# A 16-head linear attention and three further layers on one core: the first segment's way to the first products rearranged

## The reference, cut to what matters

```
qkv  = silu(x_normed @ w_qkv.T)          # 16 heads of 128, q, k, v
per block:  o = (q * q_decay) @ state + (q @ k.T * decay) @ v
            state = decay * state + (k * k_decay).T @ v
out  = rmsnorm(o);  gate = sigmoid(x_normed @ w_gate.T);  (gate * out) @ w_out.T
```

## Time and profile before

| | us |
|---|---|
| median of 3 runs | 1204.62 |
| the runs | 1197.87 to 1205.65 |
| span of the profiled execution | 1198.6 |

### The profile page before, as it was taken

One profiled execution on the slowest core, in us unless ns is written; L12 is line 12 of the kernel. 1 busy time (PEld: TensorE's weight loads), 2 busy tenths in 40 slices (PEclk: granted clock), 3 DMA queues, 4 the chain that ended last, 5 costly groups with the idle time before them and its releaser, 6 DMA issues. The chain is left out here.

```text
span 1198.6 us, 19843 instructions
## 1 busy us (share of the span) xinstructions
PE 1134.0 (95%) x7044; PEld 993.3 (83%) x7044; DVE 756.3 (63%) x1600; ACT 513.5 (43%) x969; POOL 240.8 (20%) x274
## 2 busy tenths in 40 slices
PE   5999999999999999999999996889999779989997
PEld 4988988988989889889898995667776668878897
DVE  4765665666656647657567578754445975786656
ACT  5576344344443443444434555422222356554322
POOL 1012010110100101101001002033332742322211
PEclk9999999999999999999999997899999958999999
DMA  4001001000001001001000003733333324000001
GB/s 149 10 1 36 10 1 36 9 0 35 9 0 40 4 0 44 0 0 44 0 0 1 1 2 120 228 93 106 106 106 91 95 82 146 1 1 1 19 18 36
DMA packets 29212, 50.33 MB, mean 42 GB/s; under 512 B 5122, under 2 KB 19426, under 8 KB 27874
## 3 DMA queue, kind: packets, MB, share of 16 engines
q1 hardware_dynamic: 24978, 38.68, 9.8%
q0 software_dynamic: 3840, 10.49, 3.3%
q10 hardware_dynamic: 336, 0.39, 0.1%
HBM read 36.70 MB, written 10.49 MB: 39 GB/s over the span
## 5 line engine op out<-in xcount | busy, mean ns | idle before, releaser
L635 POOL TENSOR_TENSOR linear_out_row<-linear_out_row,lin_sq 128x512 f32<-128x512 f32 x64 | 91.3, 1426 | 598.7 <-ACT lin_sq L536 595.7
L42 PE MATMUL lin_bank<-keep_xT_hi,lin_w_hi 128*128 128x512 f32 x384 | 155.4, 405 | 2.6 <-DVE keep_xT_lo L244 2.6
L591 DVE TENSOR_TENSOR lin_st<-lin_bank,lin_mask 128x512 f32<-128x512 f32 x64 | 44.3, 692 | 174.9 <-PE lin_bank L446 174.9
L43 PE MATMUL lin_bank<-keep_xT_lo,lin_w_hi 128*128 128x512 f32 x384 | 152.6, 397 | 0.0
L44 PE MATMUL lin_bank<-keep_xT_hi,lin_w_lo 128*128 128x512 f32 x384 | 152.5, 397 | 0.0
L532 ACT ACTIVATE lin_o<-lin_bank 128x512 f32<-128x512 f32 x64 | 38.3, 598 | 189.9 <-PE lin_bank L477 189.9
L473 PE MATMUL lin_bank<-lin_st,lin_v 128*128 128x128 f32 x512 | 94.0, 275 | 0.0
L42 PEld LDWEIGHTS lin_bank<-keep_xT_hi,lin_w_hi 128*128 128x128 f32 x384 | 72.9, 190 | 17.9 <-issue 3.0
L44 PEld LDWEIGHTS lin_bank<-keep_xT_hi,lin_w_lo 128*128 128x128 f32 x384 | 72.5, 189 | 17.8
L477 PE MATMUL lin_bank<-lin_qd,lin_state 128*128 128x128 f32 x448 | 87.2, 276 | 0.0
L43 PEld LDWEIGHTS lin_bank<-keep_xT_lo,lin_w_hi 128*128 128x128 f32 x384 | 72.8, 189 | 14.8
(11 more groups left out here) (395 smaller groups left out, 2775.9 us busy)
## 6 DMA issues: line engine op xcount, KB each, us to landing
lin_raw<-in_wp SPq DMA_DIRECT2D x8, 1024.0 KB, 4.8
sorted_y<-shared_loaded SPq DMA_DIRECT2D x48, 128.0 KB, 2.1
experts_up_expert_up<-in_wgu SPq DMA_DIRECT2D x16, 352.0 KB, 7.2
keep_x<-in_x SPq DMA_DIRECT2D x4, 512.0 KB, 7.3
lin_raw_out<-in_wop SPq DMA_DIRECT2D x8, 256.0 KB, 2.6
tokens_x<-linear_out_row SPq DMA_DIRECT2D x4, 512.0 KB, 10.6
linear_out_row<-in_ffn_up SPq DMA_DIRECT2D x2, 1024.0 KB, 5.9
tail_q<-tail_qT SPq DMA_DIRECT2D x28, 64.0 KB, 2.0
```

The costliest lines, as they stand in the source:

```text
L42: nc.tensor.matmul(out, lh, rh, start=first, stop=False, skip_group_check=skip)
L43: nc.tensor.matmul(out, lh, rl, start=False, stop=False, skip_group_check=skip)
L591: dve.tensor_tensor(C4(st[:, a, :]), C4(bank[2 + a][:]), mask[:, a:a + 1, :].broadcast_to([P, TPS, P]), ALU.mult).then_inc(st_sb, 1)
L635: pool.tensor_tensor(part, part, sq[:, a, :], ALU.add).then_inc(squares_sb, 1)
```

## The change

- The four tiles of segment 0 are issued as four transfers with a semaphore each, ahead of everything; the slopes are issued by ScalarE instead of SyncE. `raw` arrives in two transfers by column halves (0 to 511: q0, k0, q1, k1; 512 to 1023: g, v), both ahead of the norm weights and segment 1.
- `dve_first` takes each tile's statistics as it arrives, and normalizes tiles 2 and 3; `act_first` normalizes tiles 0 and 1. `pe_turn_first` waits for VectorE's tiles before the block that needs them.
- Both splits of the weights go by column halves, in every pass. In the first, half 0 is split before `act_high` and `dve_low`, half 1 after.
- `project_first` writes q0 of segment 0 in another order, each product waiting for its own parts: high by high for both feature halves, low weights by high, high by low. `pe_pass` waits for the second half of the weights only before v.
- The slopes' negation (L148) moves behind the second half of the weights on VectorE.
- TensorE first makes `WARM` = 12 products of the identity with itself into bank 7, which g1's first product overwrites: six whole, six in two halves of 64 output partitions each.

The diff, without the parts that only pass names on:

```diff
 RMS_EPS, LN_EPS = 1e-6, 1e-5
 PAIRS = NH // 2
 DMA = 16
+WARM = 12
 def three_passes(nc, out, lhs, rhs, first=True, last=True, skip=False):
...
     def dve_start(self, dve):
         dve.wait_ge(self.numbered, 4)
         dve.tensor_scalar(self.ages[:], self.ages[:], 0.0, None, ALU.max).then_inc(self.ready, 1)
+    def dve_slopes(self, dve):
         dve.wait_ge(self.slopes_in, DMA)
         dve.tensor_scalar(self.neg[:], self.slopes[:], -1.0, None, ALU.mult).then_inc(self.ready, 1)
...
                         z.then_inc(self.z_y_ready, 1)
                 chain.wait()
+    def dve_first(self, dve, chain, arrived):
+        at = slice(TPS, 2 * TPS)
+        for j in range(TPS):
+            dve.wait_ge(arrived[j], DMA)
+            chain.step(dve.bn_stats(self.stats[:, TPS + j, :], self.keep.x[:, j, :]))
+        chain.wait()
+        for j in range(TPS):
+            chain.step(dve.bn_aggr(self.mean_var[:, TPS + j, :], self.stats[:, TPS + j, :]))
+        chain.wait()
+        dve.tensor_scalar(self.spread[:, at], self.mean_var[:, at, 1], LN_EPS, None, ALU.add).then_inc(self.spread_ready, 1)
+        dve.wait_ge(self.root_ready, 1)
+        chain.link(dve.reciprocal(self.scale[:, at], self.root[:, at]))
+        dve.scalar_tensor_tensor(self.shift[:, at], self.mean_var[:, at, 0], -1.0, self.scale[:, at], ALU.mult, ALU.mult).then_inc(self.affine_ready, 1)
+        for j in range(TPS // 2, TPS):
+            last = dve.tensor_scalar(self.z_x(0)[:, j, :], self.keep.x[:, j, :], self.mean_var[:, TPS + j, 0:1], self.scale[:, TPS + j:TPS + j + 1],
+                                     ALU.subtract, ALU.mult)
+        last.then_inc(self.z_x_dve, 1)
+    def act_first(self, act):
+        act.wait_ge(self.affine_ready, 1)
+        for j in range(TPS // 2):
+            last = act.activation(self.z_x(0)[:, j, :], self.keep.x[:, j, :], ACT.Identity,
+                                  scale=self.scale[:, TPS + j:TPS + j + 1], bias=self.shift[:, TPS + j:TPS + j + 1])
+        last.then_inc(self.z_x_ready, 1)
+    def pe_turn_first(self, pe):
+        pe.wait_ge(self.z_x_ready, 1)
+        for k in range(KT):
+            for j in range(TPS):
+                if k == 0 and j == TPS // 2:
+                    pe.wait_ge(self.z_x_dve, 1)
+                last = pe.transpose(self.banks[k][:, j * P:(j + 1) * P], self.z_x(0)[:, j, k * P:(k + 1) * P], self.keep.ident[:])
+            last.then_inc(self.turned, 1)
     def dve_low(self, dve, g):
         for k in range(KT):
             dve.wait_ge(self.high, KT * g + k + 1)
...
                                         (keep.xT_hi[:, f, toks], keep.xT_lo[:, f, toks]), f == 0, f == KT - 1)
                 return last
-            pe.wait_ge(w_hi_done, 2 * hp + 2)
-            pe.wait_ge(w_lo_done, 2 * hp + 2)
+            def project_first():
+                cols, toks = slice(0, P), slice(0, SEG)
+                pe.wait_ge(w_hi_done, 1)
+                for f in range(KT):
+                    pe.wait_ge(norms.high, f + 1)
+                    nc.tensor.matmul(bank[0][:], w_hi[:, f, cols], keep.xT_hi[:, f, toks], start=f == 0, stop=False)
+                pe.wait_ge(w_lo_done, 1)
+                for f in range(KT):
+                    nc.tensor.matmul(bank[0][:], w_lo[:, f, cols], keep.xT_hi[:, f, toks], start=False, stop=False)
+                for f in range(KT):
+                    pe.wait_ge(norms.low, f + 1)
+                    last = nc.tensor.matmul(bank[0][:], w_hi[:, f, cols], keep.xT_lo[:, f, toks], start=False, stop=f == KT - 1)
+                return last
+            if not first:
+                pe.wait_ge(w_hi_done, 2 * hp + 2)
+                pe.wait_ge(w_lo_done, 2 * hp + 2)
             for seg in range(SEGS):
                 t = 4 * hp + seg
                 start = first and seg == 0
-                if first:
+                if first and seg:
                     pe.wait_ge(norms.low, KT * (seg + 1))
                 if not start:
                     pe.wait_ge(o_sb, 2 * t - 1)
-                project("q", 0, bank[0], seg).then_inc(q_mm, 1)
+                (project_first() if start else project("q", 0, bank[0], seg)).then_inc(q_mm, 1)
                 if not start:
                     pe.wait_ge(o_sb, 2 * t)
                 project("k", 0, bank[1], seg).then_inc(k_mm, 1)
...
                 if not start:
                     pe.wait_ge(st_sb, 2 * t)
                 project("k", 1, bank[3], seg).then_inc(k_mm, 1)
+                if start:
+                    pe.wait_ge(w_hi_done, 2)
+                    pe.wait_ge(w_lo_done, 2)
                 for b in range(2):
                     if not (first and seg <= 1):
                         pe.wait_ge(acc_sb, 2 * t - 3 + b)
...
                                         (g_hi[:, a, :], g_lo[:, a, :]), a == 0, a == 1)
                 last.then_inc(w_mm, 1)
+        HALVES = (slice(0, 512), slice(512, 1024))
         def act_split(act, hp):
             act.wait_ge(raw_in, DMA * (hp + 1))
-            for f in range(KT):
-                act.activation(w_hi[:, f, :], raw[:, f, :], ACT.Copy).then_inc(w_hi_done, 1)
+            for half in HALVES:
+                act.activation(w_hi[:, :, half], raw[:, :, half], ACT.Copy).then_inc(w_hi_done, 1)
+        def act_split_first(act, n):
+            act.wait_ge(raw_in if n else raw_half, DMA)
+            act.activation(w_hi[:, :, HALVES[n]], raw[:, :, HALVES[n]], ACT.Copy).then_inc(w_hi_done, 1)
         def act_pass(act, hp, first, last):
             for seg in range(SEGS):
...
                 chain.link(dve.tensor_copy(g_hi[:, a, :], g[:, a, :]))
                 dve.tensor_tensor(g_lo[:, a, :], g[:, a, :], g_hi[:, a, :].bitcast(F32), ALU.subtract).then_inc(g_sb, 1)
+        def dve_split_half(dve, hp, n):
+            dve.wait_ge(w_hi_done, 2 * hp + 1 + n)
+            half = HALVES[n]
+            dve.tensor_tensor(w_lo[:, :, half], raw[:, :, half], w_hi[:, :, half].bitcast(F32), ALU.subtract).then_inc(w_lo_done, 1)
         def dve_split(dve, hp):
-            for f in range(KT):
-                dve.wait_ge(w_hi_done, 2 * hp + 1 + f)
-                dve.tensor_tensor(w_lo[:, f, :], raw[:, f, :], w_hi[:, f, :].bitcast(F32), ALU.subtract).then_inc(w_lo_done, 1)
+            for n in range(2):
+                dve_split_half(dve, hp, n)
         def accumulate(dve, t, seg):
...
         with nc.Block() as block:
             @block.sync
             def _(sp):
-                decays.load(sp, slope)
                 tiles = x.rearrange("b (t p) f -> p (b t) f", p=P)
-                for g in range(SEGS):
+                for j in range(TPS):
+                    sp.dma_start(keep.x[:, j, :], tiles[:, j, :]).then_inc(x_first[j], DMA)
+                sp.dma_start(raw[:, :, HALVES[0]], w_pairs[0][:, :, HALVES[0]]).then_inc(raw_half, DMA)
+                sp.dma_start(raw[:, :, HALVES[1]], w_pairs[0][:, :, HALVES[1]]).then_inc(raw_in, DMA)
+                sp.dma_start(norm_in[:], norm_w).then_inc(norm_sem, DMA)
+                for g in range(1, SEGS):
                     at = slice(g * TPS, (g + 1) * TPS)
                     sp.dma_start(keep.x[:, at, :], tiles[:, at, :]).then_inc(x_in[g], DMA)
-                    if g == 0:
-                        sp.dma_start(raw[:], w_pairs[0]).then_inc(raw_in, DMA)
-                        sp.dma_start(norm_in[:], norm_w).then_inc(norm_sem, DMA)
                 sp.dma_start(raw_out[:], wout_pairs[0]).then_inc(raw_out_in, DMA)
                 with sp.Fori(0, PAIRS - 1) as hp:
                     sp.wait_ge(w_lo_done, 2 * hp + 2)
...
                 chain = Chain(dve, own)
                 norms_chain = Chain(dve, norms_own)
                 decays.dve_start(dve)
-                dve_norms(dve, norms_chain, 1)
-                dve_split(dve, 0)
+                norms.dve_first(dve, norms_chain, x_first)
+                dve_split_half(dve, 0, 0)
                 norms.dve_low(dve, 0)
+                dve_split_half(dve, 0, 1)
+                decays.dve_slopes(dve)
                 dve_norms(dve, norms_chain, 2)
                 dve.memset(output.ones[:], 1.0).then_inc(output.ones_ready, 1)
                 chain.link(dve.memset(keep.acc[:], 0.0))
...
             @block.scalar
             def _(act):
+                decays.load(act, slope)
                 norms.act_root(act, 1)
-                norms.act_apply(act, 1)
-                act_split(act, 0)
+                norms.act_first(act)
+                act_split_first(act, 0)
                 norms.act_high(act, 0)
+                act_split_first(act, 1)
                 norms.act_root(act, 2, split=False)
                 norms.act_apply(act, 2)
                 decays.act_start(act)
...
             @block.tensor
             def _(pe):
                 pe.wait_ge(decays.numbered, 5)
-                norms.pe_turn(pe, 0)
+                for n in range(WARM):
+                    if n < WARM // 2:
```

(5 more changed lines are left out.)

6 lines of the change are left out of this document (4 added, 2 removed).

## The result

| | before | changed |
|---|---|---|
| median, 20 runs each | 1200.49 us | 1196.76 us |
| the runs | 1197.11 to 1205.65 | 1192.91 to 1198.71 |
| span of the profiled execution | 1198.6 us | 1191.6 us |

The ratio of the changed kernel to the one before is 0.9963, with a 95% interval from 0.9953 to 0.9972: 4.4 us gained, between 3.4 and 5.6 (the two medians in the table are 3.7 apart). The forecast was 5.0. The median of the first three runs of before, 1204.62, lay 4 us above that of twenty.

The account below looks back on a forecast made before the run. TensorE, busy 95% of 1198.6 us, was taken as the bound, leaving only its start to shorten: 5.2 us arriving less 0.2 lost gives 5.0, hence 1199.6 against the 1204.62 median, taken as 1199; range 1192 to 1204.5.

Parts of the forecast that it names:

- S: Start of the kernel, moment the first segment's four statistics end: claimed 5.0 us instead of 6.6, 1.6 us gained.
- Rival A: Start: ScalarE's, little comes through; fourth tile takes 3.9 us or overwritten products end at 9.8; some 2.9 us left, 1202; chance 0.20.
- Normalization, weights, transposed parts: Start: shared normalization saves 1.0 us more before transposes; half the weights ahead of first products; seventh product about 11.2, not 17.34.
- V: Start of the products of `lin_v` and `lin_kd` (L457 before): claimed 25.85 us instead of 31.04.
- What is late next: ScalarE's fixed order behind segment 1's statistics: 2 us become a wait for ScalarE, 5.2 us arrive.
- Rival B: Start: all of TensorE's gain arrives, 7.3 us, giving 1197; needs ScalarE's exponentials or table loads out of the way; chance 0.08.
- The overwritten products: TensorE's idle start: twelve products end between 7.3 and 9.8 us; loss taken as 0.2, between nothing and 2.5.
- the 0.5 worked out: TensorE's start: if the clock rises only at 16.2 us, 4.7 us are gained instead of 5.2.
- The clock: TensorE's start: up at the seventh product gives 5.2 us; if transposes don't count and the warm-up is lost, 4.7.
- The sum's own size, 5.0: Whole kernel: 5.2 us arriving from the start less 0.2 for the overwritten products; forecast case's chance 0.50.
- Rival C: Later stages: slower, as the clock falls to 1.2 GHz in more stretches; ten such microseconds eat the gain, twenty give 1209; chance 0.15.
- Rival D: Start: the change doesn't do what it says, clock low until 25.7 us, time as before, 1204.6; chance 0.07.

Follow-up runs that it names:

- same half twice: Changed kernel with the twelve half-width overwritten products all on output partitions 0 to 63 instead of alternating halves; products of `lin_v` and `lin_kd` start at 26.60 us.
- slopes on SyncE: Changed kernel with x's first segment and the first weights in one transfer each, slopes issued first by SyncE; products of `lin_v` and `lin_kd` start at 27.30 us.
- x one, weights one: Changed kernel with x's first segment in one transfer and the first weights in one transfer; products of `lin_v` and `lin_kd` start at 30.63 us.

## Why the prediction was right, point by point

*The time.* The gain came as forecast, 4.4 us where 3.5 to 6 was said. The time of 1199 was built on a median of three runs that lay 4 us high; the measured 1196.76 is below the 1198 to 1201 that went with the forecast, and inside the wide range of 1192 to 1204.5.

*S.* Predicted 5.0, measured 5.25. The fourth tile landed 2.6 us after its issue (2.4 assumed). The price nearly stood; its reasons didn't. I counted the slopes' move as 0.46 us of SyncE and the tiles as one statistic instead of four. The runs show that each was measured wrongly by itself: the tiles with the slopes on SyncE bring 0.5 us of S (6.51 to 6.02), the slopes' move another 0.8, and the slopes' move without the tiles loses 3.2. That the sum of two wrong reasons came near is luck. Rival A had this danger as competition with the weights; in the runs it went with the slopes.

*Normalization, weights, transposed parts.* Predicted and measured: transposes 7.5 and 7.71, high weights 7.4 and 7.55, second low part 10.9 and 11.04, seventh product 11.2 and 11.44. VectorE's two tiles took 0.73 us, inside ScalarE's 1.09. One thing went unpriced: the first half of the weights landed 4.7 us after its issue, at 7.4, 0.2 before ScalarE took it up at 7.55. In the run with the same half twice it was 0.56 us too late, and V with it.

*What is late next.* Segment 1's statistics at 12.15 and 12.17, `lin_q` at 21.13 and 21.17, the transposes of `lin_k` at 22.3 and 22.31, V at 25.85 and 25.87, all in the row of ScalarE's fixed order. The run with the exponentials early showed that this order, and no other thing, keeps 1.8 us back. Rival B needed exactly this and is excluded for the change as it is.

*The overwritten products.* They ended at 7.78, transposes were ready at about the same time, and nothing was lost: 0 of the 0.2 assumed and the 2.5 feared, because the halves overlap. What they bring is up to 0.56 us (0.18 of it scatter in S), against the 0.5 worked out, and that agreement is luck. The 0.5 stood for a clock that rises at 16.2 and makes TensorE itself late; without the products it rose before 12.5, and the loss came by the transposes and ScalarE's chain. The sum was off as well: transposes of `lin_k` ready at 23.4 and the 2.66 us from there to the products of `lin_v` and `lin_kd` give 26.1, a loss of 0.2 and not 0.5.

*The clock.* Here a step was missing. I weighed the clock only as up or down at the seventh product, and took the order by parts as worth nothing beyond its place. In the run with the old order a wait of 2.61 us there is followed by a low clock from 12.2 to 15.6. The rule that transposes do not count (the Trainium skill, TensorE: Matmul & The Clock Gate, PE-mode transpose) gets no support: without any product ahead of them the transposes from 7.96 ran into products at 9.82, and the full clock was there by 12.52, where in the kernel before it came after 5.3 us of products. Three more runs have transposes at the low level that run into products; in them it came 1.8 (x in one transfer), 1.9 (slopes on SyncE) and 4.0 us (x one, weights one) after the first product. The rule is not refuted either, since the moments of the rise scatter by some 3 us from run to run (5.1 to 8.2 us in runs with the same products).

*From 5.3 to 4.4.* The sum's own size, 5.0, was met by the profile's 5.3 and by the runs' 4.4, within its interval. Rival C named the right thing at the wrong place: the clock's falls after a wait. The one that matters for the change lies at 91 us, after a wait of 2.15 us, and takes 1.0 to 1.7 us when it comes. The changed kernel's first profile doesn't have it, its second does, and that is luck of the execution. The later ones (1003 to 1010) gave this profile 1.7 us for nothing. Rival D is excluded by the steps.

## What to carry to other kernels

When a start is shortened, follow every engine's list through to the first place where two of them meet again: 7.0 us gained on TensorE's side (V at 24.09, with the exponentials out of its way) were worth 5.2, because ScalarE's exponentials, not late before, became the next bound, and moving them into its idle time gave the rest at V. Compare moments in the two profiles (one instruction near 30, 120 and 950 us), not only spans; a constant distance says where a gain was made, and a jump says where the clock played its part. Take the parts of a change apart before crediting them: here the slopes on the other queue win 0.8 us beside four small transfers and lose 3.3 beside a large one. And say which parts nobody took out: here the shared normalization and the weights by halves.

## What the runs showed of the hardware that I had not expected

- With a small broadcast transfer (128 rows of 64 bytes) issued on ScalarE's queue at the same moment as a 512 KB transfer on SyncE's, the large one landed 7.1 and 7.5 us after its issue in two runs, instead of 3.8 and 3.9 behind the small one on one queue, and the small one 6.1 and 6.7 after, instead of 2.8. Beside four transfers of 128 KB neither was late.
- TensorE's clock can fall after waits of only 2.1 to 2.6 us, in some executions and not in others of the same program: granted 0.57 against 1.00 over 91 to 95 us behind the same wait of 2.15 us. At the start, the eight transposes took 1.82 us behind a wait of 2.11 (x and weights in one transfer each, slopes on SyncE) and 1.09 behind one of 1.59 (four tiles, slopes on SyncE).
- Products of 64 outputs run in pairs, on different output partitions, at the price of one: 24 records in 1.58 us against 24 in 2.89 us on the same partitions.
